# State-space tiles: decay matrices by exponentials of summed logarithms on ScalarE instead of running products on VectorE, and the per-chunk factors of all batches made with the time steps

## The reference

```python
def segsum_exp(a):      # out[i, j] = exp(sum_{k=j+1..i} a[k]) for i >= j, else 0
    ...
A_cs = cumsum(A)                                   # within a chunk of 128 tokens, per head (8 heads)
Y_diag = einsum('bcln,bcsn,bhcls,bcshp->bclhp', C, B, segsum_exp(A), x)
decay_states = exp(A_cs[..., -1:] - A_cs)
states = einsum('bcln,bhcl,bclhp->bchpn', B, decay_states, x)    # then carried from chunk to chunk
Y_off = einsum('bcln,bchpn,bhcl->bclhp', C, states, exp(A_cs))
y = forward(Y_diag + Y_off) + backward(...) + skip terms;  y = rmsnorm(y * silu(z));  out = y @ out_proj
```

## Time and profile before

| | us |
|---|---|
| median of 3 runs | 2140.66 (2139.45 to 2144.73) |
| profiled execution, its time | 2139.38 |
| profiled execution, its span | 2137.7 |
| `mamba`, from its first DMA to the store of its last output | 88.96 to 784.04 |
| one batch of it (steady) | 82.1 |

### The profile page before, as it was taken

One profiled execution on the slowest core, in us unless ns is written; L12 is line 12 of the kernel. 1 busy time (PEld: TensorE's weight loads), 2 busy tenths in 40 slices (PEclk: granted clock), 3 DMA queues, 4 the chain that ended last, 5 costly groups with the idle time before them and its releaser, 6 DMA issues. The chain is left out here.

```text
span 2137.7 us, 33282 instructions
## 1 busy us (share of the span) xinstructions
PE 1813.6 (85%) x10026; PEld 1244.3 (58%) x10026; DVE 1499.4 (70%) x3126; ACT 1006.5 (47%) x2291; POOL 446.5 (21%) x411
## 2 busy tenths in 40 slices
PE   5279898898898879799956496999989999999898
PEld 2246666566567568699952144565646565555555
DVE  5678788888887852122226596888888888888885
ACT  2132241341341312122112153888888888888886
POOL 2122314314314332422111101001020202020101
PEclk9588899999998989999987697999999999999999
DMA  4501221221122129555525395225243434353311
GB/s 172 169 30 60 79 78 59 69 88 59 59 85 72 57 90 324 184 184 174 174 67 176 102 281 175 66 77 93 70 100 80 90 85 102 80 100 79 80 31 30
DMA packets 143788, 226.09 MB, mean 106 GB/s; under 512 B 17725, under 2 KB 110015, under 8 KB 143648
## 3 DMA queue, kind: packets, MB, share of 16 engines
q1 hardware_dynamic: 124464, 179.95, 27.7%
q0 software_dynamic: 19184, 44.45, 8.2%
HBM read 174.26 MB, written 50.99 MB: 105 GB/s over the span
## 5 line engine op out<-in xcount | busy, mean ns | idle before, releaser
L2243 DVE TENSOR_SCALAR att_scores<-att_psS 128x512 f32<-128x512 f32 x512 | 348.8, 682 | 102.5 <-PE att_psS L2075 86.2
L2192 ACT ACTIVATE att_prob<-att_scores,att_shift 128x512 f32<-128x512 f32 x512 | 383.2, 749 | 30.5 <-DVE att_shift L2259 30.5
L2201 ACT COPY att_pT<-att_psT 128x512 f32<-128x512 f32 x512 | 306.0, 599 | 132.6 <-PE att_psT L2083 130.8
L2251 DVE CUSTOM_DVE_ANT_0 att_scores<-att_scores,first_decay 128x512 f32<-128x512 f32 x512 | 347.6, 679 | 0.0
L2083 PEld LDWEIGHTS att_psT<-ident,att_prob 128*128 128x128 f32 x2048 | 245.2, 142 | 158.8 <-issue 99.8
L2083 PE MATMUL att_psT<-ident,att_prob 128*128 128x128 f32 x2048 | 315.2, 277 | 15.2 <-ACT att_pT L2201 13.7
L2075 PE MATMUL att_psS<-first_ks,first_qs 128*128 128x512 bf16 x512 | 197.6, 387 | 27.7 <-DVE att_scores L2243 23.1
L2097 PE MATMUL att_psO<-att_pT,att_v 128*32 128x512 f32 x1024 | 138.5, 615 | 37.7 <-ACT att_pT L2201 37.7
L1524 DVE TENSOR_SCALAR ffn_hT<-ffn_psH,ffn_b 128x128 f32<-128x128 f32 x156 | 44.2, 344 | 165.6 <-PE ffn_psH L1460 148.8
L1460 PE MATMUL ffn_psH<-ffn_xT,ffn_w 128*128 128x128 f32 x1248 | 150.0, 280 | 11.0 <-issue 10.5
L1460 PEld LDWEIGHTS ffn_psH<-ffn_xT,ffn_w 128*128 128x128 f32 x1248 | 149.4, 197 | 13.7 <-issue 11.9
(11 more groups left out here) (282 smaller groups left out, 2919.0 us busy)
## 6 DMA issues: line engine op xcount, KB each, us to landing
ffn_w<-in_w SPq DMA_DIRECT2D x39, 1024.0 KB
mamba_am<-a_rows SPq DMA_DIRECT2D x64, 512.0 KB, 3.6
first_qs<-q_parts SPq DMA_DIRECT2D x256, 64.0 KB
first_ks<-k_parts SPq DMA_DIRECT2D x256, 64.0 KB
xn<-xn_all SPq DMA_DIRECT2D x16, 512.0 KB, 5.7
ffn_w<-in_w POOLq DMA_DIRECT2D x8, 1024.0 KB, 6.0
att_w<-in_inter POOLq DMA_DIRECT2D x7, 1024.0 KB, 5.5
att_w<-in_outer POOLq DMA_DIRECT2D x7, 1024.0 KB
```

The source lines that it names most:

```text
L2192: nc.scalar.activation(prob[:, n % NP], scores[:, n % NCL], ACT.Exp, bias=shift[:, h % 2, t:t + 1], accum_out=total[:, octet % 2, t, j, i: ...
L2201: nc.scalar.copy(pT[:, h % HEADS_T, :, t * P:(t + 1) * P], bank_of("turn", n)[:].rearrange("p (k q) -> p k q", k=CPB)).then_inc(pT_ready, 1)
L2243: vec.tensor_scalar(scores[:, n % NCL], psS[n % NS][:], -CLAMP, CLAMP, ALU.max, ALU.min).then_inc(clipped, 1)
L2251: vec.tensor_tensor_reduce(scores[:, n % NCL], scores[:, n % NCL], decay[:, FAR - t * P:FAR - t * P + SEQ], 1.0, -2.0 * CLAMP, ALU.mult, A ...
```

## The change

- `time_steps` stores the running sums of `a` themselves, not exponentials: TensorE multiplies `a` by the strict triangle of its direction (4 matmuls in place of 4 transposes), ScalarE copies them, SP stores them. The same step makes, for all batches, three more sums (strictly before, after, and whole tile; 6 matmuls of 256 columns), of which ScalarE takes three Exps, and the negative inclusive sums `minus` (2 more such matmuls, copied by VectorE). `dt * rest` is made there too.
- In `mamba` the 6 sum matmuls, the Exp of `fac`, the `dtdec` product and the copy of `a` are gone. `steps_of` copies the batch's slices of `dt`, `dt_decay` and two `factors`; ScalarE copies the slice of `minus`.
- The 8 scans of a batch are gone. ScalarE makes `L` by `exp(am + minus)`, one activation of 128x128 for each of 8 heads with a per-partition bias, so 64 a batch. Units 0 to 4 come right after the `xl` copies, 5, 6 and 7 between squares and `yT` copies. `L` has 4 buffers instead of 3.
- Above the diagonal those exponentials are of positive sums. VectorE first multiplies `gT` by both triangles into `masked` (one 128x256 product a tile, so 4 a batch), and `decays(u)` becomes `min(L, 1) * masked`, with both inputs in SBUF.
- TensorE's `products(t)` waits for `g_masked` instead of `L_ready`; `output(0)` and `output(1)` move behind units 4 and 6; VectorE's `outputs` move one step later.
- GpSimd no longer fills `begin` and the ends of `am`.

```diff
+                pe.wait_ge(a_ready, 2)
+                for d in range(2):
+                    for g in range(2):
+                        mm = nc.tensor.matmul(psA[:, d * 2 + g], flat_heads(a[:, d, g * HALF:(g + 1) * HALF]), tri[d], start=True, stop=True)
                 mm.then_inc(a_turned, 1)
+                for d in range(2):
+                    mm = nc.tensor.matmul(psF[0][:, d], tri[1 - d], flat_heads(a[:, d]), start=True, stop=True)
+                mm.then_inc(summed, 1)
+                for d in range(2):
+                    mm = nc.tensor.matmul(psF[1][:, d], tri[d], flat_heads(a[:, d]), start=True, stop=True)
+                mm.then_inc(summed, 1)
+                for d in range(2):
+                    mm = nc.tensor.matmul(psF[2][:, d], C.ones[:], flat_heads(a[:, d]), start=True, stop=True)
+                mm.then_inc(summed, 1)
+                for d in range(2):
+                    mm = nc.tensor.matmul(psM[:, d], incl[:, d], flat_heads(a[:, d]), start=True, stop=True)
+                mm.then_inc(summed, 1)
...
+                nc.scalar.copy(aT[:], psA[:]).then_inc(aT_ready, 1)
+                act.wait_ge(summed, 1)
+                nc.scalar.activation(rest[:].rearrange("p d t h -> p (d t h)"), psF[0][:].rearrange("p d n -> p (d n)"),
+                                     ACT.Exp).then_inc(decay_ready, 1)
+                for q in range(2):
+                    act.wait_ge(summed, q + 2)
+                    nc.scalar.activation(steps.factors[:, q].rearrange("p d t h -> p (d t h)"),
+                                         psF[q + 1][:].rearrange("p d n -> p (d n)"), ACT.Exp).then_inc(factors_ready, 1)
...
+                for e in range(2):
+                    v.scalar_tensor_tensor(out=incl[:, e], in0=tri[e], scalar=-1.0, in1=C.ident[:], op0=ALU.mult, op1=ALU.subtract)
...
+                dve.wait_ge(decay_ready, 1)
+                v.tensor_tensor(steps.dt_decay[:], steps.dt[:], rest[:], ALU.mult)
+                dve.wait_ge(summed, 4)
+                v.tensor_copy(steps.minus[:].rearrange("p d t h -> p (d t h)"), psM[:].rearrange("p d n -> p (d n)")).then_inc(minus_ready, 1)
+                dve.wait_ge(minus_ready, 1)
...
-    NA, NL = 4, 3
...
-                    row = ((i * CPB + u // 2) * 2 + u % 2) * NH
-                    sp.dma_start(am[:, v % NA, 1:1 + NH * P],
+                    row = ((u % 2) * NT + i * CPB + u // 2) * NH
+                    sp.dma_start(am[:, v % NA],
                                  a_rows_d[row:row + NH, :].rearrange("h t -> (h t)").unsqueeze(0).to_broadcast([P, NH * P])
                                  ).then_inc(am_in[v % NA], 16)
...
-                    pe.wait_ge(ab_ready, i + 1)
-                    for q in range(3):
-                        for d in range(2):
-                            lhs = C.ones if q == 2 else tri[d] if q == 0 else tri[1 - d]
-                            at = (q * 2 + d) * CPB * NH
-                            mm = nc.tensor.matmul(sums[:, at:at + CPB * NH], lhs[:], ab[:, d], start=True, stop=True)
-                    mm.then_inc(sums_ready, 1)
...
-                    pe.wait_ge(fac_ready, i + 1)
+                    pe.wait_ge(fd_ready, i)
...
-                        pe.wait_ge(L_ready, i * U + (2 * t - 2 if t >= 2 else 0))
+                        pe.wait_ge(g_masked, i * CPB + (t - 1 if t >= 2 else 0))
...
                         if u in (4, 6):
                             turn_tile(u // 2 - 2)
+                        elif u in (5, 7):
                             output(u // 2 - 2)
...
+                def decays(i, u):
+                    t, d = u // 2, u % 2
+                    if u >= NL:
+                        act.wait_ge(diag_used, i * U + u + 1 - NL)
+                    else:
+                        act.wait_ge(diag_used, i * U)
+                    act.wait_ge(am_in[u % NA], (i * (U // NA) + u // NA + 1) * 16)
+                    for h in range(NH):
+                        ex = nc.scalar.activation(L[:, u % NL, h], am[:, u % NA, h * P:(h + 1) * P], ACT.Exp, bias=minus[:, d, t, h:h + 1])
+                    ex.then_inc(decayed, 1)
...
-                    act.wait_ge(sums_ready, i + 1)
-                    act.wait_ge(off_scaled, i * 6)
-                    nc.scalar.activation(fac[:].rearrange("p a b c h -> p (a b c h)"), sums, ACT.Exp).then_inc(fac_ready, 1)
+                    act.wait_ge(decayed, i * U)
+                    nc.scalar.copy(minus[:], steps.minus[:, :, bass.ds(i * CPB, CPB), :]).then_inc(minus_ready, 1)
...
-                    for t in range(CPB - 1):
-                        squares(i, t)
-                        turned_tile(i, t)
+                    act.wait_ge(minus_ready, i + 1)
+                    for u in range(NL):
+                        decays(i, u)
+                    decays(i, 4)
+                    squares(i, 0)
+                    decays(i, 5)
+                    turned_tile(i, 0)
+                    decays(i, 6)
+                    squares(i, 1)
+                    decays(i, 7)
+                    turned_tile(i, 1)
+                    squares(i, 2)
+                    turned_tile(i, 2)
...
-                    pool.wait_ge(dtdec_ready, i + 1)
+                    pool.wait_ge(steps_ready, i + 1)
...
                 def steps_of(i):
-                    dve.wait_ge(sums_ready, i)
                     dve.wait_ge(xdt_ready, i * U)
-                    for d in range(2):
-                        v.tensor_copy(dtb[:, d], dt[:, bass.ds(i * CPB, CPB), d * NH:(d + 1) * NH])
-                        cp = v.tensor_copy(ab[:, d], a[:, bass.ds(i * CPB, CPB), d * NH:(d + 1) * NH])
-                    cp.then_inc(ab_ready, 1)
+                    dve.wait_ge(xdd_ready, i * 6)
+                    dve.wait_ge(off_scaled, i * 6)
+                    v.tensor_copy(dtb[:], steps.dt[:, :, bass.ds(i * CPB, CPB), :])
+                    v.tensor_copy(dtdec[:], steps.dt_decay[:, :, bass.ds(i * CPB, CPB), :])
+                    for q in range(2):
+                        cp = v.tensor_copy(fac[:, q], steps.factors[:, q, :, bass.ds(i * CPB, CPB), :])
+                    cp.then_inc(steps_ready, 1)
...
-                    def products_of(u):
-                        t, d = u // 2, u % 2
-                        if u >= NL:
-                            dve.wait_ge(diag_used, i * U + u + 1 - NL)
-                        else:
-                            dve.wait_ge(diag_used, i * U)
-                        dve.wait_ge(am_in[u % NA], (i * (U // NA) + u // NA + 1) * 16)
-                        at = 0 if d == 0 else 2
-                        back = -1 if d else 1
-                        v.tensor_tensor_scan(L[:, u % NL].rearrange("p h t -> p (h t)")[:, ::back],
-                                             am[:, u % NA, at:at + NH * P][:, ::back],
-                                             begin[:, d].rearrange("p h t -> p (h t)")[:, ::back], 0.0,
-                                             ALU.mult, ALU.add).then_inc(decayed, 1)
-                    for u in range(NL):
-                        products_of(u)
-                    dve.wait_ge(ab_ready, i + 1)
-                    dve.wait_ge(fac_ready, i + 1)
-                    dve.wait_ge(xdd_ready, i * 6)
-                    v.tensor_tensor(dtdec[:], dtb[:], fac[:, 1], ALU.mult).then_inc(dtdec_ready, 1)
+                    dve.wait_ge(steps_ready, i + 1)
...
-                        dve.wait_ge(g_ready, i * CPB + t + 1)
+                        if d == 0:
+                            dve.wait_ge(g_ready, i * CPB + t + 1)
+                            dve.wait_ge(L_ready, i * U + (2 * t - 2 if t >= 2 else 0))
+                            v.tensor_tensor(masked[:, t % 2], gT[t % 2], C.triangles[:], ALU.mult).then_inc(g_masked, 1)
+                            dve.wait_ge(g_masked, i * CPB + t + 1)
                         dve.wait_ge(decayed, i * U + u + 1)
-                        v.tensor_tensor(L[:, u % NL], L[:, u % NL], gT[t % 2][:, d].unsqueeze(1).to_broadcast([P, NH, P]), ALU.mult).then_inc(L_ready, 1)
+                        v.scalar_tensor_tensor(out=L[:, u % NL], in0=L[:, u % NL], scalar=1.0,
+                                               in1=masked[:, t % 2, d].unsqueeze(1).to_broadcast([P, NH, P]),
+                                               op0=ALU.min, op1=ALU.mult).then_inc(L_ready, 1)
...
-                        if u + NL - 1 < U:
-                            products_of(u + NL - 1)
-                        if u >= 5 and u % 2 == 1:
-                            outputs((u - 5) // 2)
+                        if u >= 6 and u % 2 == 0:
+                            outputs((u - 6) // 2)
```

115 lines of the change are left out of this document (57 added, 58 removed).

## The result

The changed kernel takes 2111.09 us (median of 4 runs, 2110.75 to 2115.85), the one before 2140.93 (median of 4, 2139.45 to 2144.73): ratio 0.9863, interval 0.9844 to 0.9882, so 29.8 us less; the forecast was 2124, which is the 16.5 us less that the prediction added up, taken from the profiled execution's 2139.4, plus 1.3. The profiled execution is the slowest of the four (2115.85, span 2114.1); the spans of the other three are 2109.0 to 2109.4.

What follows compares the result with a forecast made beforehand. TensorE was taken to bound the kernel, gains coming only from its idle time and dropped work. Per batch -2.56, eight batches -20.5, `time_steps` +4: -16.5 from 2139.4 gives 2122.9, plus 1.3 for the median: 2124 us, range 2104 to 2144.

Steps and rivals of the forecast that it cites:

- the `Bl` wait: Batch entry, x transposes on TensorE: the wait for ScalarE's `Bl` copies shrinks from 1.35 to 0.6 us, -0.75 a batch.
- the exchange of waits: Diagonals in `mamba`: `L` and `yT` waits go (-1.5 - 1.5), two new `y_read` waits come (+2.0); -1.0 us a batch.
- sum matmuls: Batch entry on TensorE: six small matmuls ahead of the B transposes go, -1.26 us a batch.
- Exp, one step: ScalarE making `L`: 0.26 to 0.41 us per exponential, 0.3 taken; units 0 and 1 ready in time, at nothing.
- `y_read` of tile 0: TensorE's wait for VectorE's read of tile 0: 2.0 us falls to 1.45, -0.55 a batch.
- new `y_read` waits: Units 4 and 6 on TensorE wait for `y_read` after their turn, 0.95 to 1.0 us, twice a batch.
- waits for `L` and `yT`: TensorE's waits for `mamba_L` (1.5 us) and for the `yT` copy (1.5) both go in each batch.
- port: Grow phase: VectorE's product with two SBUF inputs and GpSimd's `xdd` hold each other up, +1.0 us a batch (0 to +2.2).
- `time_steps`: Ahead of `mamba`: eight further matmuls and a pass lengthen the path once by +1.8 to +5.4 us, +4 taken.
- a rival with 18.7: Clock gains: the two low-clock stretches in each batch go, 18.7 us more saved, 2105 us; chance 0.17.
- The port as a rival: Units 3, 5 and 7 each meet a GpSimd instruction, half not covered: 12 us back, 2136 us; chance 0.15.
- ScalarE's (2151): At 0.6 us an Exp, unit 1 is 3.4 late in each batch, +27 us, 2151; chance 0.04.

Runs made afterwards that it cites:

- first group's chip: The chip that ran `after_again`, `factors_alone`, `output_back` and `masked_psum` together with the kernel before, whose median there was 2138.59 us.
- the factors alone: Against the changed kernel: scans, three `L` buffers and old order stay; factors made with the time steps, sum matmuls and batch's Exp gone; 2113.60 us, ratio 0.9882.

## Why the prediction was right, and where not

The engine and the place were right: TensorE bounds the batch, what leaves VectorE is no saving by itself, and the gain is the matmuls, the `Bl` wait and the exchange of waits. By its steps, for the batch 454.40:532.57 against the earlier trace rows:

| step | forecast | measured |
|---|---|---|
| sum matmuls | -1.26 | gone, B transposes follow `z` |
| wait at the x transposes | 1.35 to 0.6 | 1.35 to 0.43 + 0.19 = 0.62 |
| Exp, one step | 0.3 | 0.295 |
| `y_read` of tile 0 | 2.0 to 1.45 | 2.0 to 1.38 |
| new `y_read` waits | 0.95 to 1.0, twice | 0.94, twice |
| waits for `L` and `yT` | both gone | both gone |
| port | +1.0 | `xdd` wait +0.2, in others +0.7; with `masked` in PSUM -1.2 |
| a batch | -2.56 | -3.3 in the mean |
| `time_steps` | +4 | +4.9 (+5.4 and +3.0 in the other traces) |
| last batch | -2.56 | +0.1 |
| clock | unchanged | -10.5 over three batches |

Each wait but the port's came out within 0.1 us. What was off:

- **A batch, 0.75 more.** 0.4 of it is in TensorE's busy time (72.37 to 70.73 is -1.64, of which 1.26 are the matmuls); the rest is the port, entered at 1.0 as an addition. Its price is real (1.2 to 1.4 by the run with `masked` in PSUM), but the kernel before already waited 1.6 for the same `xdd`, which there met `scaled` (1.20 where 0.72 is usual), so only 0.2 to 0.7 was new. The step that failed is taking a price for a difference.
- **The last batch, 2.6 less.** The prediction gave it the same gain as the others. It has no convolution, and moving `outputs(1)` behind `finish(3)` made a wait of 2.2 that the prediction didn't name.
- **The clock, 10.5.** It had been a rival with 18.7, from two low stretches a batch. Their number stayed (0.96 in both kernels), though the one behind the `Bl` wait went, as the rival had it, and another came: in 375.60:454.40 one begins 22 us behind the start, soon after the wait for `xdd`; in 454.40:532.57 one of nearly 7 us stands for both. What went were the three batches at 0.88 to 0.90. Only one execution of before was traced; that its other runs had such batches too is suggested by the granted clock over the whole program (0.926 to 0.931 in its runs on the first group's chip, 0.932 to 0.937 in the changed kernel's there) and not shown.
- **`time_steps`, 0.9.** The eight further matmuls are recorded as 16 instructions of 256 columns that end at 92.1, within the bounds 90.0 to 93.6 given; the time from the last pass to the first DMA is the rest. The other two traces of the changed kernel (+5.4 and +3.0) show that 0.9 is within what executions differ by.

The sum: -16.5, then -5.2 (seven batches by 0.75), -10.5 (clock), +2.6 (last batch), +2.0 (up to the first `zs`) and +4.0 (unchanged code, cause open) is the -23.6 of the profiled execution; its sisters are 4.9 shorter, and before's median stands 1.5 above its profiled execution. So the clock's 10.5 is more than the whole 7.1 by which the traced difference missed the forecast's 16.5, and the forecast came this near because misses of both signs met. That much of it is luck; the mechanism of the steady batch is not. The port as a rival (2136) and ScalarE's (2151) fell: at 0.295 an Exp the units were ready in time, and it took twice as many to make TensorE wait. Where the second low stretch will fall and how many batches run low, the prediction couldn't tell from its rows.

What the prediction left out is what the scans' move is worth. It entered -1.0 for the exchange of the `L`, `yT` and `y` waits; the run with the factors alone shows that with the port's price, the clock and the outputs' place nothing of it is left in the change as built. The one with the outputs put back shows that it was worth 12.6 us, and the one with `read_y` first that 31 us lay behind one instruction's place in VectorE's queue. By the prediction's own terms the outputs' move cost 0.5 a batch (waits of 1.5 for two of 1.0), and it was not asked what keeping their place would give. The 2 x 0.68 us that it worked out for `y_read` were the hint: two passes ahead of a release, of which only one had to be.

The Exps agree to 1 ns with the Trainium skill, ScalarE: Activation LUTs, section What ACT_TABLE_LOAD costs (280 ns + 0.833 ns a column gives an estimate of 387 for 128, less 93 of 294; the trace has 388 and 295). The rule of the Trainium skill, SBUF — State Buffer, section SBUF: two separate sides, that GpSimd and a VectorE instruction with two SBUF inputs lock each other out, agrees with 1.22 against 1.56, and with 1.21 once one input lay in PSUM.

## What to carry to other kernels

Work taken off an engine that isn't the bound shows only where the bounding engine waits for it: list those waits first, and look at the order in the relieved engine's queue, for the release of a buffer (here `read_y`) should stand ahead of all that nobody waits for. When a change has parts, time each alone: here the factors alone gave as much as the whole. The larger part, the scans' move, gained 12.6 us, and a later place of the outputs that was bundled with it took them away again; with one line moved in VectorE's queue the scans' side was 1.8% ahead. And check the last round of a loop by itself, since the work that covers a wait in the others may not be in it.

## What the runs showed of the hardware

- The granted clock can undo a gain in TensorE's waits. Two batches of one kernel with the same instructions and the same waits took 74.59 at 1.00 and 83.43 at 0.88 of 2.4 GHz; in the second the level was 1.2 GHz behind a wait of 1.86 us, and 16 matmuls of 128x64 took 3.5 to 3.7 instead of 1.90; in the first, behind the same wait, it was 2.4 (1.00). What decides between the two stays open. Once the 3.3 us of `y` waits were gone (and the outputs' place on VectorE changed) a batch ran at 0.98 (72.15) with that wait still in it.
- Code that no one touched took different times: the stages behind `mamba` 1355.0 to 1359.5 us in four kernels on one chip, with TensorE busy 1172.4 to 1178.7 at equal counts. On two other chips they took 1335.8 to 1342.3, with TensorE busy 1166.9 to 1176.0; what makes the 18 us isn't known.
- Chips differ by about half of what the change brings: the kernel before took 2138.59 on one, 2124.70 and 2125.67 on two others (0.7%), while the ratio of the change to it was 0.9867 on the first and 0.9868 on the last.
- A VectorE product of 128x1024 with both inputs in SBUF took 1.22 us alone and 1.56 beside a GpSimd instruction, and 1.21 in the same place with one input in PSUM. Two `xdd` took 2.04 alone and 2.49 beside `scaled`, a product with both inputs in SBUF.
